# Second layer's attention: four heads per slot in 32-row tiles, f32 scores, bf16 maxima

## The reference, cut to what matters

```
q = rope(heads(x @ W_q.T + b_q));  k = rope(heads(x @ W_k.T + b_k));  v = heads(x @ W_v.T + b_v)
scores = einsum('bhtd,bhsd->bhts', q, k);  mask = where(tril, 0.0, -inf)
probs = softmax((scores + mask) / sqrt(8));  out = einsum('bhts,bhsd->bhtd', probs, v) @ W_o.T + b_o
h = gelu(einsum('ecd,edf->ecf', xe, W1) + b1);  ye = einsum('ecf,efd->ecd', h, W2) + b2
```

## Time and profile before

| | |
|---|---|
| median of 3 runs | 2048.22 us (2047.69 to 2049.31) |
| the profiled execution | 2053.99 us, its span 2052.1 us |
| mean granted clock | 0.891 |
| PE, DVE, ACT, POOL busy | 82%, 60%, 44%, 37% of the span |
| prepare / project1 / experts / attend1 of layer 2 | to 1286 / 1343 / 1513 / 2052 us |

### The profile page before, as it was taken

How to read it: one execution, slowest core, us unless ns; L and a number is a source line. 1 busy time by engine, 2 the same in 40 slices (tenths; PEclk the granted TensorE clock), 3 DMA queues, 4 the chain that set the end, 5 groups by cost and what they waited for, 6 DMA issues and landing times. The chain is left out here.

```text
span 2052.1 us, 35695 instructions
## 1 busy us (share of the span) xinstructions
PE 1683.1 (82%) x13083; PEld 838.5 (41%) x13083; DVE 1229.1 (60%) x2140; ACT 901.6 (44%) x1457; POOL 768.6 (37%) x423
## 2 busy tenths in 40 slices
PE   2777798798989988899899972459988889898988
PEld 2455354353544535454353432236633333323333
DVE  5422876758675675766766506811357766676573
ACT  0112265364554635546454540213235655455455
POOL 1502745556475663755657671710035000000000
PEclk9998699899998999999999985679979988798688
DMA  4122200000000000000000001233310000000000
GB/s 155 52 81 85 44 12 11 7 22 7 23 12 13 17 10 21 12 18 12 12 19 7 17 6 57 86 105 103 93 41 23 21 27 27 28 2 27 27 1 21
DMA packets 59157, 69.96 MB, mean 34 GB/s; under 512 B 13274, under 2 KB 42862, under 8 KB 58094
## 3 DMA queue, kind: packets, MB, share of 16 engines
q1 hardware_dynamic: 54894, 59.31, 9.3%
q0 software_dynamic: 4096, 8.40, 1.5%
HBM read 43.48 MB, written 19.53 MB: 31 GB/s over the span
## 5 line engine op out<-in xcount | busy, mean ns | idle before, releaser
L1480 POOL TENSOR_TENSOR a_prob_sum<-a_prob_sum,a_prob 128x1024 f32<-128x1024 f32 (+2 forms) x224 | 499.4, 2230 | 236.4 <-ACT a_prob L1428 215.5
L1428 ACT ACTIVATE a_prob<-a_st,a_table 128x512 f32<-128x512 f32 (+3 forms) x640 | 352.7, 626 | 355.3 <-PE a_st L1306 218.1
L1918 DVE TENSOR_REDUCE a_maxima<-a_mx 128x1 f32<-128x512 f32 (+3 forms) x640 | 351.5, 604 | 148.1 <-PE a_mx L1906 107.7
L1526 DVE TENSOR_REDUCE a_maxima<-a_ring 128x16 f32<-128x512 f32 (+3 forms) x640 | 352.8, 600 | 128.9 <-PE a_ring L1238 101.5
L2175 ACT ACTIVATE a_prob<-a_st 128x1024 f32<-128x1024 f32 (+1 forms) x320 | 271.5, 899 | 228.7 <-PE a_st L2075 130.1
L1333 PE MATMUL a_ot<-a_prob,a_values 128*64 128x512 f32 (+3 forms) x1280 | 287.8, 568 | 0.0
L1238 PE MATMUL a_ring<-a_k_hi,a_q_hi 64*128 64x512 f16 (+3 forms) x640 | 165.3, 374 | 92.0 <-DVE a_maxima L1526 69.2
L1906 PE MATMUL a_mx<-a_ks,a_qs 49*128 49x512 bf16 (+3 forms) x640 | 181.5, 393 | 43.1 <-DVE a_maxima L1918 41.7
L2091 PE MATMUL a_ot<-a_prob,a_values 128*32 128x512 f32 (+3 forms) x1280 | 184.7, 633 | 0.0
L1306 PE MATMUL a_st<-a_q_hi,a_k_hi 64*128 64x512 f16 (+4 forms) x704 | 135.1, 339 | 0.0
L2075 PE MATMUL a_st<-a_qs,a_ks 49*128 49x512 bf16 (+3 forms) x640 | 129.9, 401 | 6.1 <-issue 2.4
(11 more groups left out here) (249 smaller groups left out, 2681.8 us busy)
## 6 DMA issues: line engine op xcount, KB each, us to landing
a_rden<-rden_wide SPq DMA_DIRECT2D x64, 128.0 KB, 2.9
f_w<-in_w SPq DMA_DIRECT2D x28, 256.0 KB, 2.8
expert_in<-zeros SPq DMA_DIRECT2D x5, 1024.0 KB, 9.8
f_rows<-expert_in SPq DMA_DIRECT2D x16, 256.0 KB, 3.3
a_values<-values_all SPq DMA_DIRECT2D x8, 512.0 KB
expert_out<-f_result SPq DMA_DIRECT2D x16, 256.0 KB, 2.4
shared_w<-in_w SPq DMA_DIRECT2D x12, 256.0 KB, 3.0
parts<-p_part_t SPq DMA_DIRECT2D x6, 512.0 KB, 2.7
```

The costliest lines, as they stand in the source:

```text
L1428: e = act.activation(prob[:, s % NPROB, a, c0:QW], ps_st[s % 2][:, a, c0:QW], ACT.Exp, bias=table[x][:, a, at:at + 1])
L1480: pool.tensor_tensor(into[:, :, c0:QW], into[:, :, c0:QW], here[:, :, c0:QW], ALU.add).then_inc(added, 2 if r == TPQ - 2 else 1)
L1526: dve.reduce_max(maxima[:, qt // TPQ, a, qt % TPQ, at:at + count], bank[:, 0:hi - lo].rearrange("p (w k) -> p w k", k=WINDOW), AX_X).then_ ...
L1918: dve.reduce_max(own.maxima[:, qt // TPQ, a, qt % TPQ, n:n + 1], bank[:, 0:hi - lo], AX_X).then_inc(done, 1)
```

## The change

Four heads make a group (`HPG1 = 4`), so there are 4 groups of 40 slots, again 160 slots. A slot is one key tile by 512 queries for four heads, each on a 32-row tile of the array. The score operands are now f32: row 32a holds minus the maximum (ones in the keys), the next 8 the features; the other 23 rows hold zeros (in q) and are multiplied all the same. Scores are one f32 matmul per head over all 512 columns, also on the diagonal. The maxima use bf16 operands of their own (`qb`, `kb`), 8 rows of data in 32, one part only. The mask of a diagonal tile is added in four 32-row steps per head rather than two of 64, from four copies of the table that are turned by 32 rows each. The split into bf16 parts in project1 is gone: q and k are turned in f32, ACT takes out f32, DVE bf16. The values are read from `values_all` and not loaded per group. The maxima of group 0 (now four heads) run along the last two steps of the experts. attend1 is written out in full, with no loop. A turn's row is stored by 4 DMAs, a group's operands by 16.

```diff
-SLOTS1 = [(qb, m) for qb in range(NQB) for m in range(TPQ * (qb + 1) // 2)]
+SLOTS1 = [(qb, kt) for qb in range(NQB) for kt in range(TPQ * qb + TPQ)]
...
+        begun = final - (1 if beside else 0)
+        units = 2 * FC * step_blocks * (final - begun + 1)
...
+def load_operands1(sp, own, x, g):
+    for a in range(HPG1):
+        features = slice(DH1 * (HPG1 * g + a), DH1 * (HPG1 * g + a) + DH1)
+        wide, narrow = slice(32 * a + 1, 32 * a + 1 + DH1), slice(32 * a, 32 * a + DH1)
+        for k, (dst, dst_b) in enumerate(((own.qs, own.qb), (own.ks, own.kb))):
+            sp.dma_start(dst_b[x][narrow, :], own.parts_b[k, features, :]).then_inc(own.loaded[x], 16)
+            sp.dma_start(dst[x][wide, :], own.parts[k, features, :]).then_inc(own.loaded[x], 16)
...
 class FirstMaxima:
     def gpsimd(self, pool):
-        set_ones1(pool, self.own, 1)
+        fill_narrow1(pool, self.own, 0)
+        fill_narrow1(pool, self.own, 1)
+        fill_wide1(pool, self.own, 1)
     def clear(self, dve):
-        set_ones1(dve, self.own, 0)
+        fill_wide1(dve, self.own, 0)
...
+            def scores(g, s, half):
+                (qb, kt), c0 = SLOTS1[s], first_col(s)
+                diag = kt >= TPQ * qb
+                two = (2 * half, 2 * half + 1)
+                for a in two:
+                    mm = pe.matmul(ps_st[half][:, a % 2, :], ks[g % 2][rows_of(a), P * kt:P * kt + P],
+                                   qs[g % 2][rows_of(a), QW * qb:QW * qb + QW], start=True, stop=not diag)
+                for h in range(4 if diag else 0):
+                    for a in two:
+                        wide = 32 * h + 32
+                        select, mask = quarter(mem, a, h, 3 * P, 3 * P + wide)
+                        mm = pe.matmul(ps_st[half][:, a % 2, c0:c0 + wide], select, mask, start=False, stop=h == 3)
                 mm.then_inc(st_full, 1)
...
+            for slot in slots1():
+                n, g, s = slot.n, slot.g, slot.s
+                if slot.chunk:
...
+                    maxima_of(slot.chunk, 0)
+                if n < ALL1:
...
+                    for half in range(2):
+                        if n >= 1:
+                            pe.wait_ge(exp_done, 2 * n - 1 + half)
+                        scores(g, s, half)
+                if slot.chunk:
+                    maxima_of(slot.chunk, 1)
+                for kind, (whose, qb), at in slot.others:
+                    unit(kind, whose, qb, at)
+                if 1 <= n <= ALL1:
+                    weighted(n - 1)
```

More of the change, by code:

```diff
@@ L644, in step @@
                 after = None
[L645 to L646 removed]
+                if is_along(i):
+                    places = places_of(i, blocks)
                     def after():
[L649 removed]
+                        beside.tensor(pe, mem, next(places), units)
                 for n in range(blocks):
@@ L1666 @@
-PROJ_AT1 = {NS1 + 7: 0, NS1 + 11: 1, NS1 + 17: 2, 2 * NS1 + 1: LAST_QB}
+OUT_AFTER1, TRANS_AFTER1, PROJ_AFTER1, TAIL1 = 3, 5, 7, 6
 RING1 = 3
-PRODUCTS1 = 32
-ROWS1 = PRODUCTS1 + 1 + 2 * DH1
+MAX_ORDER1 = (2, 3, 0, 1)
+ROWS1 = 32
 FOLD1 = DH1 + 1
-HEAD_LOADS1 = 9
-GROUP_LOADS = 2 * HEAD_LOADS1 + 1
+HEAD_LOADS1 = 4
+GROUP_LOADS = HPG1 * HEAD_LOADS1
 SCALE1 = float(1 / np.sqrt(np.float32(DH1)))
[L1676 to L1695, removed]
+@dataclass
@@ L1696, in units1, with slots1 @@
+class Slot1:
+    n: int
+    g: int
+    s: int
+    chunk: tuple
+    others: list
+def slots1():
+    at, out = TURNS_BEFORE1, []
+    for n in range(ALL1 + TAIL1):
+        g, s = divmod(n, NS1)
+        chunk, others = None, []
+        if g < GROUPS and s < len(LATE1):
+            chunk = (g, LATE1[s], at)
+        elif g + 1 < GROUPS and s >= len(LATE1):
+            chunk = (g + 1, EARLY1[s - len(LATE1)], at)
+        at += HPG1 if chunk else 0
+        if s in TURN_AT1 and n > 0:
             ahead, qb = TURN_AT1[s]
-            if not (first and n == 0) and (more or not ahead):
-                one.append(("turn", (x + ahead, qb), at))
+            if g + ahead < GROUPS:
+                others.append(("turn", (g + ahead, qb), at))
@@ L1722, in project1 @@
+        out.append(Slot1(n, g, s, chunk, others))
+    for kind in ("trans", "proj"):
+        if not any(o[0] == kind and o[1][1] == LAST_QB for slot in out for o in slot.others):
+            out[-1].others.append((kind, (GROUPS - 1, LAST_QB), at))
+            at += 1
+    return out
+def project1(nc, mem, dram, parts, parts_b, values_all):
     with ExitStack() as ctx:
@@ L1910, in max_pair1 @@
     if diag:
-        for mm in mask_queries(pe, mem, [bank[:, hi - lo - P:hi - lo] for bank in banks]):
-            mm.then_inc(full, 1)
+        for h in range(4):
+            for a, bank in zip(heads, banks):
+                select, mask = quarter(mem, a, h, P + 32 * h, 2 * P)
+                mm = pe.matmul(bank[:, hi - lo - P + 32 * h:hi - lo], select, mask, start=False, stop=h == 3)
+                if h == 3:
+                    mm.then_inc(full, 1)
 def max_reduce1(dve, own, a, c, bank, full, wanted, done):
@@ L2131, in step @@
[L2131 to L2149 removed]
+            turned_at = {}
```

580 lines of the change are left out of this document (252 added, 328 removed).

## The result

| | before | after |
|---|---|---|
| median | 2047.95 us (2044.33 to 2049.31, 4 runs) | 2028.14 us (2022.21 to 2030.89, 4 runs) |
| profiled execution, its span | 2053.99, 2052.1 us | 2022.21, 2019.3 us |
| mean granted clock | 0.891 | 0.932 |

The ratio is 0.9902, with a 95% interval of 0.9874 to 0.993: 20 us faster, where 53 were forecast. The two profiled executions differ by 31.8 us, since that of before lies 6 us over its median and that of after 6 us under its own. What follows is read from these two, so its sum is 32.8 us of span.

A forecast was written before the change was run, and what follows sets the result against it. It took a ring of waits between PE and DVE in attend1, plus time at the lower clock, to bound the kernel. Attend1's slots -52, first turns +1, project1 -10, experts' start -2, maxima +10: -53, so 1995 us, range 1950 to 2085.

The forecast's parts named there:

- Diagonal slots: attend1, 64 of 160 slots: 2.7 us each (2.5 to 3.0), with DVE's 2.5 covering full-width scores and extra masks.
- The rival of the hand-over: attend1: second pair of scores issues only when the first is done, slots 3.2 to 3.3 us, 2091 us; chance 0.15.
- Plain slots: attend1, slots off the diagonal: 2.7 us each again, bounds 2.5 (DVE alone) and 3.3.
- The loop of ACT and scores: attend1: score pairs and exponentials wait on each other, two slots in 5.24 us, 2.62 each, level with DVE.
- the rival of slow row tiles: attend1: four f32 row tiles slow each other, 0.26 us more per slot, 42 in all, 2037 us; chance 0.08.
- Outputs and turns: attend1: 16 outputs units at 1.25 make 20 us; turns 13 x 0.3 = 4; transposes and projections 5.
- The -4 for the last group's slots without maxima: attend1: 24 slots without maxima, held at 2.6 us by the new loop, diagonal ones near 2.0: -4 us.
- The clock: attend1: 40 us at 1.2 GHz in place of 172, because the array streams more, a loss of 14 us (0 to 60).
- project1: project1: scatters no longer slowed by DVE's casts and subtractions, -10 us (-11 to -4).
- Start of the experts: Experts' start: DVE's fills +1 us, rows of block 2 landing sooner -3, together -2 (-8 to +5).
- The extra step: Experts: 24 pairs of maxima in each of the last two steps, before only in the last: +10 us (7 to 16).
- The signs named ahead: Profile: slots 2.7 us apart, DVE idle below 100, clock over 0.92; wrong if over 3 us or ACT's waits pass 130.

The follow-up runs named there:

- masks_last: The changed kernel with the score masks of diagonal slots queued behind the scores of all four heads: 1992.8 us, 0.9703 of the kernel before.
- no_score_masks: The changed kernel with the score masks of the diagonal blocks left out, so part of the output differs: 1975.0 us, 0.9598 of the kernel before.
- masks_first: The changed kernel with each head's masks ahead of its f32 product in diagonal slots, over used columns only: 1981.3 us, 0.9648 of the kernel before.
- Narrow scores: The changed kernel with f32 scores in diagonal slots over the used columns only: 1990.4 us, 0.9684 of the kernel before.
- nine rows: The changed kernel with 9 rows in place of 32 in scores and maxima, without the rows of zeros: 2351.2 us, 1.1468 of the kernel before.

## Why the prediction was wrong

The direction was right, and so was the loop of the plain slots; the price of the diagonal slots was not, and the gain was 20 us for 53. By its own steps, in the profiled executions:

- **Diagonal slots** are the step that failed: "with eight mask matmuls in place of four for each pair (320 columns, 0.13 us)", taken at 2.7 with bounds 2.5 to 3.0. They took 3.30, of which outputs, turns and the like, which the sum has as terms of their own, are 0.14. Without these it is 3.16: 64 x 0.46 = 29 us. The masks were costed by what they stream and not by what they wait for. The rival of the hand-over named this very thing, "a queue that does not pass it while mask matmuls wait", and its 3.2 to 3.3 us a slot is what came; but it was put on all 160 slots or on none, and masks are in 64. Split by kind of slot it would have come out right: some 2.6 us in 96 slots and 3.2 in 64. masks_last, no_score_masks and masks_first show it. The trace of before had a sign of it: the prediction read 130 us of ACT's waits for scores, and another 98 us had ended with a mask.
- **Plain slots** were forecast at 2.7 and take 2.61 without units: -9 us. The loop of ACT and scores at 2.62 holds: all four heads end 1.1 us after the second pair's issue (1700.56 to 1701.68). In masks_last both pairs of one slot issue 0.15 us apart (1674.32 and 1674.46) and the second still ends 1.1 us after its issue, so four f32 row tiles do run side by side, and the rival of slow row tiles falls.
- **Outputs and turns**: plain slots with an outputs unit take 1.3 more than those without, 1.25 forecast, and in all the outputs cost 1.5 us less than the 20 in the sum. Turns, transposes and projections took some 4 us more than forecast. (The split of before has no term for the last two; their 5 us lie in the 62 that it put down to the clock.) The -4 for the last group's slots without maxima lies in the means above, so as a term of its own it goes: +4.
- **The clock**: forecast 40 us at 1.2 GHz for a loss of 14. It was 20.5 us at the start, for a loss of some 4 (two slots of 5.15 and 5.32 us), and 10 after the last exponential. That the clock rises came true by luck: "the array streams more" was not the reason. Narrow scores stream less and the clock stays; nine rows stream the same and it goes. What held it lower in the kernel before, with its 49 rows of bf16 per head, no run tested.
- Together 29 - 9 - 1.5 + 4 + 4 - 10 = 16.5 us, for the 15 between -52 and -36.6; the last slot ends with its exponentials and is some 2 us shorter than a full one.
- **project1**: -7 for -10. No scatter of 3.28 us is left, but five of 1.70 to 1.97, beside DVE's rotation; four are followed 2.26 us after their start and not 1.26, one 2.00, so they cost 4.7 us, where -10 had left about 1 for all slow scatters. Two of them, beside two plain ones:

```profile
1302.88 0.96 POOL L440 DMA_INDIRECT expert_in<-y,slot_to  x1 [0.30 <-issue]
1304.15 1.97 POOL L440 DMA_INDIRECT expert_in<-y,slot_to  x1 [0.30 <-issue]
1306.42 0.96 POOL L440 DMA_INDIRECT expert_in<-y,slot_to  x1 [0.30 <-issue]
1307.68 1.97 POOL L440 DMA_INDIRECT expert_in<-y,slot_to  x1 [0.30 <-issue]
```

- **Start of the experts**: forecast -3 for the rows of block 2, measured -3.1 (27.0 to 23.9). **The extra step** of maxima: +14.2 (33.3 to 47.5) for +10, within its bounds of 7 to 16.
- Beyond attend1's slots the sum thus missed 3 us in project1, 4 in the step, 1 in the last step and some 2 from the last gelu to the first exponential (3.3 for 1); the +1 for DVE's filling at the start of the experts did not come. The 4.0 us ahead of project1 are scatter of stages that the change leaves alone. The medians differ by 12 us less than the profiled executions, and two traces can't say in which stage.

The signs named ahead came so: slots 2.7 apart only off the diagonal, where they were over 3 us at full clock, the first sign against; clock 0.97; the last two steps alike (47.5, 47.1). The two on waits were set by rows that leave out the waits ended by masks. DVE's idle time, 103, is not under 100, but before it was 131 by the same count. ACT's waits for scores, 204, are over "those 130 us", but before they were 228 by the same count: they fell, and this sign, as it was meant, did not come.

## What to carry to other kernels

In these traces a matmul that waited for its own rows held up ready matmuls on other rows behind it in PE's queue, and its signal came no sooner than the end of those ahead. So cost short accumulating products by what they wait for, try them first in the accumulation, and forecast kinds of slots one by one. And when a wait is read from a list, add up all rows of the waiting instruction, whatever ended them.

Before a full-height operand of zeros is trimmed as waste, look at the granted clock with and without it. And work laid beside another stage was cheapest here when spread thin: its price per piece went up with its density.

## What the runs showed of the hardware

- With equal instructions, columns and order and PE in an instruction 99% of the time, f32 products on 9 of 32 rows ran at 1.2 GHz for 785 us on end; on 32 rows, 23 of them zeros, at 2.4 GHz after 20.5 us.
- Of an f32 product's two passes on a row tile, the second issues about 0.53 us after the first; matmuls on other rows behind it can begin between them (masks at 1657.67 in masks_last, between first passes at 1657.62 and second passes at 1658.16).
- A mask of 4 x 128 f32 columns by GpSimd's affine select takes 0.635 us, and DVE's reductions beside it keep their length.
- GpSimd issues a plain DMA of eight rows in 0.50 us, SP in about 0.35 (0.3 and a gap). Eighteen small loads ahead of a stage's own in SP's queue cost that stage 11 us in these runs.
- A mask whose matmul had ended by 1658.0 released its exponential only at 1658.87, after the end of matmuls ahead of it on other rows (masks_last).
